# A graph convolution's scatter on one core: the clearing of a segment's cells stands one low group later in ScalarE's order

## The reference, cut to what matters

```
x = x + gnn(layernorm(x))                    # x: (12500, 256)
x = x + experts(layernorm(x))                # 8 experts, 256 wide

def hconv(x, src, dst, ew, w1, b1, w2, b2, g, b):
    h = relu(x @ w1 + b1)
    msg = ew[:, None] * h[src]               # 200,000 edges, dst sorted, dense at low nodes
    agg = segment_sum(msg, dst, num_segments=x.shape[0])
    h = agg @ w2 + b2
    return relu(bn(h, g, b))
```

## Time and profile before

| | |
|---|---|
| median of 3 runs | 4843.56 us (4843.49 to 4847.84) |
| span of the profiled execution | 5228.2 us |
| first layer's hot part (low groups) | about 170 to 1360 us of the span |
| ScalarE busy over the span | 2435.6 us (47%) |
| TensorE busy over the span | 4623.3 us (88%) |

### The profile page before, as it was taken

One profiled execution on the slowest core, in us unless ns is written; L12 is line 12 of the kernel. 1 busy time (PEld: TensorE's weight loads), 2 busy tenths in 40 slices (PEclk: granted clock), 3 DMA queues, 4 the chain that ended last, 5 costly groups with the idle time before them and its releaser, 6 DMA issues. The chain is left out here.

```text
span 5228.2 us, 71544 instructions
## 1 busy us (share of the span) xinstructions
PE 4623.3 (88%) x25508; PEld 3800.6 (73%) x25508; DVE 2688.7 (51%) x6606; ACT 2435.6 (47%) x4218; POOL 2110.6 (40%) x2284
## 2 busy tenths in 40 slices
PE   6778888888999579888988988649999999999999
PEld 5667777666677467776666666548888888888888
DVE  7666666566333464522222222366666666666665
ACT  4655556666211263300000000057777777777777
POOL 1466666566666456666666666630000000000000
PEclk9889999999999789999999999779999999999999
DMA  5467777566755247876666666431111111001110
GB/s 155 148 210 271 243 240 245 188 211 217 236 198 201 77 141 268 277 243 218 218 219 205 226 212 224 131 96 25 30 28 33 33 33 33 24 26 33 33 28 15
DMA packets 546618, 770.23 MB, mean 147 GB/s; under 512 B 149720, under 2 KB 441411, under 8 KB 546262
## 3 DMA queue, kind: packets, MB, share of 16 engines
q1 hardware_dynamic: 328176, 382.01, 21.7%
q0 software_dynamic: 100944, 273.96, 16.4%
q10 hardware_dynamic: 117142, 109.65, 6.5%
HBM read 605.58 MB, written 147.26 MB: 144 GB/s over the span
## 5 line engine op out<-in xcount | busy, mean ns | idle before, releaser
L1106 PE MATMUL pf<-work 128*128 128x330 f32 (+4 forms) x3528 | 1251.9, 491 | 63.3 <-DMA work<-front 31.3
L1054 POOL DMA_INDIRECT wst<-h,src_col x1040 | 1000.3, 962 | 541.9 <-issue 275.0
L1106 PEld LDWEIGHTS pf<-work 128*128 128x128 f32 x3528 | 661.0, 197 | 402.2 <-issue 220.1
L2096 DVE TENSOR_TENSOR f_hl<-f_hf,f_hh 128x1024 fp32r<-128x1024 f32 (+1 forms) x400 | 479.7, 1199 | 636.3 <-ACT f_hf L1959 636.0
L1952 ACT ACTIVATE f_hh<-f_p,f_sh,f_sc 128x512 fp32r<-128x512 f32 (+1 forms) x800 | 571.7, 768 | 395.9 <-PE f_p L2194 394.5
L1273 ACT ACTIVATE ah<-agg 128x1024 fp32r<-128x1024 f32 (+1 forms) x50 | 51.8, 1037 | 1464.2 <-DVE agg L1420 1086.6
L1138 PEld LDWEIGHTS ps<-oh,wst 128*128 128x128 f32 x4160 | 543.4, 203 | 144.5 <-issue 99.6
L1138 PE MATMUL ps<-oh,wst 128*128 128x128 f32 x4160 | 560.7, 288 | 88.6 <-issue 55.1
L1054 POOL DMA_INDIRECT f_xr<-h,src_col x518 | 497.7, 961 | 282.8 <-issue 134.0
L1054 POOL DMA_INDIRECT f_u<-h,src_col x512 | 491.1, 959 | 260.5 <-issue 136.7
L1959 ACT ACTIVATE f_hf<-f_p,f_sh,f_sc 128x512 f32<-128x512 f32 (+1 forms) x800 | 572.5, 775 | 0.0
(11 more groups left out here) (285 smaller groups left out, 7648.0 us busy)
## 6 DMA issues: line engine op xcount, KB each, us to landing
work<-h SPq DMA_DIRECT2D x216, 512.0 KB
work<-front SPq DMA_DIRECT2D x50, 924.0 KB
front<-agg ACTq DMA_DIRECT2D x12, 3300.0 KB
work<-front SPq DMA_DIRECT2D x50, 756.0 KB
work<-front SPq DMA_DIRECT2D x50, 660.0 KB
work<-front SPq DMA_DIRECT2D x50, 580.0 KB
front<-agg ACTq DMA_DIRECT2D x8, 2600.0 KB
work<-front SPq DMA_DIRECT2D x25, 832.0 KB
```

The costliest lines, as they stand in the source:

```text
L1054: g.indirect_dma_start(G[t % R], None, h_dram[layer], bass.IndirectOffsetOnAxis(ap=src_col[:, col:col + 1], axis=0)).then_inc(ga[t % R], 16)
L1106: ins = g.matmul(pF[:, k, 0:count * w].rearrange("p (s c) -> p s c", c=w), HB[a % 2][0:r, n, k * P:(k + 1) * P], x, start=b == 0, stop=b = ...
L2096: g.tensor_tensor(hlo[l][q % 2][:, :, 0:nn], hf[l][:, :, 0:nn], hhi[l][q % 2][:, :, 0:nn].bitcast(fp32), ALU.subtract).then_inc(f_lo[l], 1)
```

## The change

One number in `clears_behind`. The list of low groups behind which the pieces of segment m's clear stand begins at `begun[m - 1] + 3` and no longer at `begun[m - 1] + 2`; it still ends at `begun[m]` or after four entries, and never begins behind `begun[m]`. The number of pieces is the length of that list, and the cells are shared out evenly. The order of TensorE, VectorE, GpSimd and SyncE is the same, row for row; ScalarE has 2009 rows for 2029. The second layer's segments have two low groups, so nothing moves there.

```diff
                             for m in range(2, len(made)):
-                                at = list(range(min(begun[m - 1] + 2, begun[m]), begun[m] + 1))[:CLEARS]
+                                at = list(range(min(begun[m - 1] + 3, begun[m]), begun[m] + 1))[:CLEARS]
                                 if n in at:
                                     some.append((m, at.index(n), len(at)))
                             return some
```

## The result

The changed kernel takes 4821.81 us at the median of 5 runs, the kernel before 4845.99 us in the same sessions. The ratio is 0.9947, with a 95% interval of 0.9935 to 0.9959: faster by 24 us.

What follows compares the result with a forecast made beforehand. TensorE was taken as nearest to the bound in the first layer's aggregation, with clears in ScalarE's slack. Terms 0 - 2.9 + 1.0 = -1.9 us, taken as -2 from 4843.56, gave 4841.5 us, range 4828 to 4853.

Steps and rivals of the forecast that it cites:

- (a): ScalarE's clears in the first layer: 71 pieces become 51, same cells, some 4 us less busy time at most, costed at nothing.
- The figure of 1.9 us: Further gain from 20 fewer ScalarE instructions at 0.093 us each, if ScalarE were saturated; the prediction said it isn't.
- (b): Last clear piece against VectorE's first add into the segment: longer pieces still end in time, no VectorE wait, cost nothing.
- the cost of nothing: The cost given to VectorE's first adds: no wait for a clear, so no time lost.
- The reserve of 3.5 us: Segment m = 2: last piece ends at 258.2, VectorE's first add runs at 261.76, 3.5 us to spare.
- (c): First clear piece waiting for a store's transfer: one TensorE stand near 1034 goes, -2.9 us; the other nine waits gain nothing.
- the 2.9 us: TensorE's stand until 1034.52 for a low group behind a piece waiting for its store; forecast to go, -2.9 us.
- the rival "faster": TensorE faster, transfers unchanged: half of 31.4 us of store waits reaches TensorE and is removed, -16 us, 4828; chance 0.17.
- (d): Clearing of free cells behind m = 18's last piece, 4.28 us, moves a group later: TensorE's stand 0.55 becomes 1.5, +1.0 us.
- tighter by 7% on the whole: Scaling from the profiled 5228.2 us to the timed 4843.56 us, 0.926; the sum was taken as -2 us there.
- The sum itself, -1.9 us: Total over the first layer's aggregation: 0 - 2.9 + 1.0 = -1.9 us on the profiled 5228.2 us.

Runs made afterwards that it cites:

- the second trace of before: The kernel before, unchanged, profiled once more on a chip of the first kind: 4835.52 us, with a span of 4833.7 us.

## Why the prediction was wrong

**(a) The pieces: right as far as the runs can tell.** 51 pieces, and no gain clear of the stands from fewer instructions (0.9989, with one stand of 3.9 us gone, and 1.0009). The figure of 1.9 us that the prediction took from the Trainium skill, "Perfetto Trace Analysis", section "Optimizing Scalar/DVE Operations", was tied to a saturated engine. ScalarE is busy 705.04 of 1020 us in the window of after, and no run here shows such a gain; one of 1.9 us is too small for these intervals to exclude.

**(b) VectorE's first add: right in size, wrong in margin.** I gave every segment over 1 us ahead of the store and over 2.4 ahead of the add. In the trace after, the clear of m = 2 ends past its store and VectorE does wait:

```profile
240.39 5.70 ACT L1184 ACTIVATE agg<-zero_col 128x6600 f32<-128x6600 f32 x1
244.35 0.39 ACTq L1193 DMA_DIRECT2D front<-agg  x1
```

```profile
246.22 0.87 DVE L1339 TENSOR_TENSOR agg<-agg,px 128x686 f32 x1 [0.46 <-ACT agg L1184]
```

Three such waits are 1.6 us together, so the cost of nothing stands. The reserve of 3.5 us that I read off was that of another pace.

**(c) The waits for the stores: the step that failed.** "The other nine of the ten waits for a transfer in the earlier trace rows delay a low group too, but TensorE was not standing for it; there the gain is nothing." In the second trace of before there are 19 such waits of 118.5 us, and four of them reach TensorE with 19.5 us; the 2.9 us that I took off was one of these four (there 4.73 us). The mechanism was the right one, and it was even priced: the rival "faster" said that a faster TensorE against unchanged transfers would bring more of these waits to light, and gave it 0.17 and 16 us. It measured 24 us.

The waits were also misread in the trace that I had. I took the 28.6 us "<- issue" of ScalarE's pieces in the earlier trace rows for waits for nothing named. They are waits for stores too, for which the profile names no releaser. The largest of the six, at the first piece of m = 12:

```profile
584.50 0.37 ACTq L1193 DMA_DIRECT2D front<-agg  x1
...
606.41 1.58 ACT L1184 ACTIVATE agg<-zero_col 128x1650 f32<-128x1650 f32 x1 [11.23 <-issue]
```

The piece starts 21.91 us behind the store. In the second trace the same piece, named as waiting for the store, starts 23.09 us behind it. The other five (m = 2, 3, 5, 13 and 17) start 14.4 to 22.1 us behind their stores, four of them within 1.8 us of their distance in the second trace; m = 3 has no wait there. The trace of before lacks the times of many signals: it has them for 368 of the 518 adds of L1420, the second trace for all. So the trace of before had 60.0 us of waits for stores in 16 places, and the bound of the rival "faster", made from 31.4 us, was half of what it should have been.

**(d) The free cells: mis-sized.** I put the stand behind them at 0.55 us before and 1.5 after, +1.0 us. Measured on chips of the first kind: 1.69 us before (at low group 67), 3.36 after (at 68), +1.7 us; on the second kind 0.55 and 0.88.

**The scale: the root of (c).** I read the gap between 5228.2 and 4843.56 us as "tighter by 7% on the whole" and carried the sum over almost unchanged. It is not spread evenly. The last store stands at 1342.1 us in the trace of before and at 1195.2 us in the second one: from 170 us on the hot part is 13% shorter. The experts' stage is as long in both, 1739 us from its first product to its last (L2194). A low group comes sooner, while a store takes no less time to land: the first piece of m = 18 starts 17.69 us behind its store in the trace of before and 21.03 in the second, that of m = 19 16.46 and 17.29. For pieces that wait for a store with two low groups of reserve that is the difference between 60.0 and 118.5 us of waiting. The sum itself, -1.9 us, was made for the chip that left the trace, and there it lies inside the interval, 0.9986 (0.9973 to 0.9998), or 1 to 14 us. That the stands too went down by 1.9 us is in part luck: the 2.88 us at 1034.52 went as forecast, the stand behind the free cells grew by 0.3 and not 1.0, and the rest are small stands elsewhere. The time that was asked for was another chip's. The sign was in the numbers shown: a span 8% above every timed run.

What stays open: the last stores of the two traces are 23.3 us apart, the stands 19.3 us, the spans only 15.7 us. These are single executions, and that of before was itself 13.6 us under the median of the kernel before on its chip (4849.09 us). In the trace after the first store, ahead of anything that the change moves, is already 2.9 us later, and behind the hot part the places drift by some 8 us more. That remainder is not divided.

## What to carry to other kernels

A wait for a transfer in an in-order engine costs what is queued behind it. Put the waiting instruction behind the work that others need soonest, as late as its own consumer allows; here one low group later was enough, two were no better, and one earlier cost 2.5%. Ahead of a sum, set the span of the trace against the timed runs; where they differ by several per cent, waits of the trace that depend on a pace against a transfer's time can't be carried over, and the rival that says so deserves the larger chance. Where a wait has no releaser named, measure its end from the event that the program waits for before you call it a wait for nothing.

## What the runs showed of the hardware

The same program takes 4846 to 4849 us on three chips and 5253.56 on another. Single instructions of ScalarE and GpSimd take as long on both: a step of low parts is 390 ns, a gather's issue 964 and 962 ns. TensorE is busy longer on the slower chip, 4624.5 us for 4478.8, at a mean granted clock of 0.950 for 0.969 (the changed kernel in both); no run shows whether that is a cause or a result of its longer pauses. What clearly differs is how soon another engine goes on when TensorE has finished. A product and the add that waits for it, on the first kind (trace after):

```profile
1353.50 1.95 PE L1138 MATMUL ps<-oh,wst 128*128 128x128 f32 x16
...
1355.58 0.31 DVE L1420 TENSOR_TENSOR agg<-agg,ps 128x148 f32 x1 [3.10 <-PE ps L1138]
```

The product ends at 1355.45, the add starts at 1355.58, 0.13 us later. On the second kind (the changed kernel again, 5243.8 us), VectorE and GpSimd wait for the same product:

```profile
1510.33 1.95 PE L1138 MATMUL ps<-oh,wst 128*128 128x128 f32 x16
...
1515.11 0.30 DVE L1420 TENSOR_TENSOR agg<-agg,ps 128x144 f32 x1 [7.37 <-remote]
1515.25 0.95 POOL L1054 DMA_INDIRECT wst<-h,src_col  x1 [2.52 <-remote]
```

It ends at 1512.28, the add starts at 1515.11, 2.83 us later, and the gather at 1515.25. Over all adds into agg of gathered tiles for which VectorE had been idle for over 0.5 us, the median of this distance is 0.13 us in the trace after (368 adds) and 2.03 us here (381 adds); in the trace of before it is 2.02 us. In the other direction nothing differs: where TensorE waits for VectorE's add into the cells, its product starts 0.147 us behind that add at the median on both (24 and 119 places). The same holds in the experts' stage, which has no gathers: ScalarE (L1952) starts 0.04 us behind TensorE's product on both, and the stage takes 1739.9 and 1739.7 us from its first product to its last. So of the places compared the late ones are those where gathers run beside, and the whole difference between the two kinds lies ahead of the experts.

What makes the release late on that chip no run here shows. The ends of products are modelled in the profile, so a product that really ends later than its record would look the same. That the late release makes the hot part longer there, and hides waits for stores by giving every transfer more time, fits these rows but is argued; no experiment changed it alone.
